# Loading ScalarE's function tables ahead of a step's waits instead of behind them

## The reference

```
x = x + tanh(g_xattn[0]) * L0_xattn(layernorm(x), ctx)   # top-32-of-77 cross attention, 4 heads; FiLM; a state-space
                                                         # convolution over 512 positions; a GELU network; layer norms
x = x + tanh(g_ffn[0])   * L0_ffn(layernorm(x))          # two butterfly networks with a GELU between them
x = x + tanh(g_xattn[1]) * L1_xattn(layernorm(x), ctx)   # softmax attention, 16 heads of 8
x = x + tanh(g_ffn[1])   * L1_ffn(layernorm(x))          # 8 experts, best 2 of them, silu(u) * v
return x
```

## Time and profile before

| | |
|---|---|
| median of 3 runs | 367.29 us (366.8 to 367.44) |
| span of the profiled execution, first to last instruction | 365.1 us |
| mean granted TensorE clock in it | 0.911 of full speed |
| busy: PE, DVE, ACT, POOL | 298.4, 262.1, 209.0, 138.0 us |
| table loads on ACT | 28, together 35.9 us |

### The profile page before, as it was taken

How to read it: one execution, slowest core, us unless ns; L and a number is a source line. 1 busy time by engine, 2 the same in 40 slices (tenths; PEclk the granted TensorE clock), 3 DMA queues, 4 the chain that set the end, 5 groups by cost and what they waited for, 6 DMA issues and landing times.

```text
span 365.1 us, 5331 instructions
## 1 busy us (share of the span) xinstructions
PE 298.4 (82%) x1518; PEld 149.1 (41%) x1518; DVE 262.1 (72%) x1201; ACT 209.0 (57%) x430; POOL 138.0 (38%) x212
## 2 busy tenths in 40 slices
PE   1652100779997899999789999989999999899995
PEld 0320000639654357544544542544432444532541
DVE  3998599999799999679998882586413458801762
ACT  3799851062225465597535486544786945575560
POOL 0398998488874935443165007140000000000000
PEclk9995555658969999999999999999999999999998
DMA  7960000000000000000000000000000000000001
GB/s 246 415 238 0 1 1 0 4 1 2 0 1 1 3 0 2 2 0 1 0 2 1 1 0 2 0 2 1 0 2 0 0 3 29 0 2 3 29 19 39
DMA packets 2912, 9.56 MB, mean 26 GB/s; under 512 B 579, under 2 KB 580, under 8 KB 2628
## 3 DMA queue, kind: packets, MB, share of 16 engines
q1 hardware_dynamic: 2884, 9.23, 6.7%
HBM read 8.18 MB, written 1.05 MB: 25 GB/s over the span
## 4 chain that ended last, share of the span: by engine, by line
PE 57%; DVE 28%; POOL 6%; ACT 5%; issue 2%; DMA 1%; POOLq 0%; DVEq 0%; ACTq 0%
PE bank L461 56%; DVE R L1128 8%; DVE V L1119 5%; DVE arena L1034 4%; DVE MT L1034 3%; ACT arena L781 2%; POOL MT L1399 2%; POOL AO L1399 1%; DVE KT L1353 1%; POOL arena L1399 1%; ACT RS L781 1%; ACT L778 1%; DVE arena L1042 1%; DVE XG L1042 1%; DMA pack_kgen<-in_kgen 1%
## 5 line engine op out<-in xcount | busy, mean ns | idle before, releaser
L781 ACT ACTIVATE arena<-bank 128x512 f32<-128x512 f32 (+3 forms) x75 | 38.4, 572 | 22.3 <-PE bank L461 13.4
L778 ACT ACT_TABLE_LOAD x28 | 35.9, 1283 | 25.0 <-PE bank L461 14.0
L1128 DVE MATCH_REPLACE8 R<-V,R 128x77 f32<-128x77 f32 x192 | 40.5, 221 | 0.0
L461 PE MATMUL bank<-LO,pack_first 128*128 128x512 f32 x48 | 28.1, 677 | 15.0 <-ACT LO L781 15.0
L1456 POOL TENSOR_SCALAR sel<-R 128x308 f32<-128x308 f32 x16 | 17.7, 1107 | 37.8 <-DVE R L1128 33.1
L1119 DVE MAX8 V<-R 128x8 f32<-128x77 f32 x192 | 31.2, 223 | 0.0
L1092 DVE TENSOR_REDUCE pack_bfly<-bank 128x4 f32<-128x308 f32 x64 | 26.0, 468 | 7.2 <-PE bank L461 7.1
L461 PE MATMUL bank<-M,XN 128*128 128x308 f32 x32 | 12.8, 485 | 21.1 <-DVE XN L1034 19.8
L461 PE MATMUL bank<-arena,pack_dft 128*128 128x256 f32 (+1 forms) x96 | 29.2, 454 | 0.1
L781 ACT ACTIVATE E<-bank,negm 128x77 f32<-128x77 f32 x64 | 15.4, 326 | 15.9 <-DVE negm L1038 15.9
L781 ACT ACTIVATE LO<-bank 128x512 f32<-128x512 f32 x20 | 12.0, 600 | 21.6 <-PE bank L461 21.6
(11 more groups left out here) (208 smaller groups left out, 714.0 us busy)
## 6 DMA issues: line engine op xcount, KB each, us to landing
pack_bfly<-in_bfly SPq DMA_DIRECT2D x1, 2420.0 KB, 10.3
pack_dft<-in_dft SPq DMA_DIRECT2D x1, 1536.0 KB, 13.8
X<-in_x SPq DMA_DIRECT2D x4, 256.0 KB, 12.4
out_x<-X SPq DMA_DIRECT2D x4, 256.0 KB, 2.0
pack_ffn<-in_ffn SPq DMA_DIRECT2D x1, 512.0 KB, 14.3
pack_first<-in_first SPq DMA_DIRECT2D x1, 474.0 KB, 5.0
pack_moe<-in_moe SPq DMA_DIRECT2D x1, 452.0 KB, 15.7
pack_att<-in_att SPq DMA_DIRECT2D x1, 413.0 KB, 15.2
```

The lines of the kernel that those rows point to most:

```text
L461: return nc.tensor.matmul(out, lhsT, rhs, start=start, stop=stop, **kw)
L778: nc.scalar.add_instruction(mybir.InstLoadActFuncSet(name=nc.get_next_instruction_name(), act_func_set_id=need, ins=[], outs=[]))
L781: return nc.scalar.activation(out, in_, func, **kw)
L1128: nc.vector.match_replace(R8[:, g % 2, r % 2, h, :], V8[:, g % 2, h, r, :], src, NEG)\
```

## The change

Each step of ScalarE gets, before its waits are emitted, the table of its first function that needs one. `leads` names that function for the steps that have one; the part of `a` that loads a table becomes a function `have`, which is called at the head of each step and still from `a`. `s_cols` (Tanh), `s_kgen0` (Exp) and `units1` (Silu) are not found in `leads`, so a load that they need stays where it was.

```diff
             table = [None]
 
-            def a(out, in_, func, **kw):
+            leads = {"var": ACT.Ln, "score": ACT.Exp, "keyA": ACT.Exp, "normA": ACT.Ln, "top2": ACT.Exp,
+                     "ffn_up": ACT.Gelu, "fold_up": ACT.Gelu, "units0": ACT.Silu, "s_trig": ACT.Tanh,
+                     "s_qsin": ACT.Sin, "s_psin": ACT.Sin, "s_qexp": ACT.Exp, "s_pexp": ACT.Exp}
+
+            def have(func):
+
                 need = table_of.get(func, table[0])
                 if need != table[0]:
                     nc.scalar.add_instruction(mybir.InstLoadActFuncSet(
                         name=nc.get_next_instruction_name(), act_func_set_id=need, ins=[], outs=[]))
                     table[0] = need
+
+            def a(out, in_, func, **kw):
+                have(func)
                 return nc.scalar.activation(out, in_, func, **kw)
...
                 tile = int(step[-1]) if step[-1].isdigit() else 0
                 g = NT * b + tile
+                have(leads.get(step if step in leads else step.rstrip("012345")))
                 if step == "center2":
```

## The result

The changed kernel takes 364.2 us (median of 14 runs, 363.48 to 367.79), the kernel before in the same sitting 367.12 us (14 runs, 366.66 to 369.76). The ratio, which goes by all runs and not by the two medians, is 0.9939, with a 95% interval of 0.9912 to 0.9965: 2.2 us faster, give or take 1.0. The medians lie 2.9 us apart, because eight runs of the changed kernel took 363.5 to 364.3 us and six took 366.1 to 367.8, while 13 of the 14 of the kernel before took 366.7 to 367.7. Forecast were 1.11 us and 366.2 us, with a range of 364.8 to 367.4. The direction was right and the size too small. The profiled execution spans 361.7 us, 3.4 us less than that of before.

The account below looks back on a forecast made before the run. PE was taken to bound the kernel, busy 82% of the span, with few table loads on the last chain. Gains of 1.00 and 0.11 us made 1.11 us: 367.29 to 366.2 us, range 364.8 to 367.4.

Parts of the forecast that it names:

- Site 1: Load at 313.42, keyA0 of batch 2: hidden in ACT's 2.04 us wait, PE's expand of batch 1 gains 1.00 us.
- Site 2: Load at 141.51, score2 of batch 2: PE's idft wins 0.43 us but then waits for DVE; nothing (bounds 0 and 0.43).
- Site 3: Tail, top2 and units0 of batch 3: both loads moved, PE's transposes of the gates 0.11 us earlier (bounds 0 and 0.11).
- The other loads: The other 12 loads: nothing, those after 189 lying under a PE without a gap; uncovered, each at most 1.28 us.
- Rival 1: Last four PE passes: three or four run at full clock, 1.2 to 1.6 us more gain, 364.6 to 365.0 us; 12%.
- Rival 2: Between 316 and 348: a DVE or ACT run not hanging on PE covers the gain, 366.8 to 367.3 us; 17%.
- Rival 3: Tail passes from 352.30 on: clock falls earlier, 0.42 us per pass, up to 4.2 us, 370.4 us, slower; 8%.
- Rival 5: Table switches on ACT: each holds ACT longer than its record, hidden in idle time before; 366.8 us; 3%.

Follow-up runs that it names:

- keyA alone: Changed kernel with only the keyA entry left in `leads`, so two loads move, those at 269 and 313; 365.01 us, ratio 0.9932 to the kernel before.
- the tail alone: Changed kernel with only top2 and units0 loading ahead of their waits (five loads); 366.9 us, ratio 0.9988 to the kernel before.
- small fill: One matmul of 512 columns, read by nobody, added in PE's last pause: on the kernel before 366.16 us, on the changed kernel 363.72 us.
- a load too many: Changed kernel with one extra load of an unused table ahead of the load of keyA0 of batch 2; 365.46 us, ratio 0.9953 to the kernel before.
- four entries of thirteen: Changed kernel with only keyA, ffn_up, top2 and units0 loading ahead of their waits; 363.70 us, ratio 0.9926 to the kernel before.
- ffn_up alone: Changed kernel with only ffn_up loading ahead of its waits (four loads); 366.44 us, ratio 0.9974 to the kernel before.
- everything but keyA: Changed kernel with the loads of keyA back behind their waits; 366.5 us, ratio 0.9995 to the kernel before.
- units1: Changed kernel with units1 (Silu) added to `leads`, moving the load at 287 too; 364.15 us, ratio 0.9945 to the kernel before.

## Why the prediction was right in direction and short in size

*Site 1, the term that carried the forecast.* The mechanism was right in each part: the load right behind the copy, 0.75 us of idle time left, expand 1.01 us earlier for 1.00. The term was mis-sized behind it. I had let the score passes of scoreA3 "follow PE at 1.00 us earlier". But they wait for exponentials two to four as well, and those came the full 1.28 us earlier; in the trace of before they, and not PE's pace, had released the later passes: the third matmul of scoreA3 and the pass at 316.84 start right after the fourth exponential, whose bank that matmul takes, ends at 316.77 (314.71 and 2.06 us). So PE won 0.22 us more there (316.84 to 315.12 is 1.72, 0.22 over the 1.50 at expand), and the site is worth 1.22 us. keyA alone repeats it: 1.00 us at expand, 1.21 us behind it. I had worked out the release of the first bank and taken it for all four.

*Site 2.* Right. PE wins its 0.43 us, and DVE's run takes them back, in the timeline of PE and then of DVE after:

```profile
142.40 1.02 PE L461 MATMUL bank<-LO,pack_first 128*128 128x512 f32 x2
143.26 3.62 PE L461 MATMUL bank<-pack_dft,arena 128*128 128x256 f32 x16
...
147.98 1.13 PE L461 MATMUL bank<-X,pack_first 128*128 128x512 f32 x2 [0.21 <-DVE X L1051]
149.31 1.13 PE L461 MATMUL bank<-XG,pack_first 128*128 128x512 f32 x2
```

```profile
148.56 0.69 DVE L1043 TENSOR_TENSOR XG<-XG,XN 128x512 f32<-128x512 f32 x1
```

idft starts 0.66 us earlier (143.92 to 143.26), of which 0.22 are the scatter that was there before. The step at 149.31 is 0.22 us earlier, as DVE's product at 148.56 is the earlier trace rows, and a new wait of 0.21 us for DVE stands at 147.98.

*Site 3.* Right: 0.11 us, and 0.12 with the tail alone.

*The other loads.* Here a step failed: "nothing" for the load at 209.71, because PE is busy 47.40 of 47.40 us around it and each shape keeps its own spacing. It hid 0.3 us. Matmuls on few rows run beside each other in these traces (four passes of 12 rows with 0.38 us each take 0.56 us together), so records of two shapes overlap and cover a wait of one of them. Here the wait was that of the fourth matmul of 32 rows for its bank, and it was passed on: at 213.97 three passes of 12 rows, then one of 32 rows at 214.01 with 0.59 us, and the fourth of 12 rows only at 214.44. There was no gap in the busy time, and the four passes took 0.85 us from start to end; with the loads of ffn_up moved they take 0.56 (213.95).

*Rivals.* Rival 1 came true in the profiled execution, on top of the forecast. Its price was right (1.2 to 1.6 us said, 1.52 measured), and by the rows its chance of 12% was low. The fact to hold against "the fall may move with PE's own work" stood in the trace: it came within 0.3 us of the step's start, and the forecast moved that start by over 1 us. Rival 2 did not happen: DVE idles 0.54 us at 315.32 for 0.52 worked out. ACT idles the same 1.36 us at 316.81 as before, where I had 0.36 us left: I had moved PE earlier and left ACT's own exponentials where they were, though they moved by more than PE did. Rival 3 did not happen in the changed kernel's profile, but the profile of the changed kernel with the small fill has it, a stretch at a clock of 0.50 from 350.5 to 353.8 (stretch, length, PE busy, clock, DMA share, GB/s, PE alone):

```profile
350.50:353.80 3.30, 3.30 (x5) 0.50 0.00 0
...
359.70:361.60 1.90, 1.90 (x5) 1.00 0.00 0
```

So it was a case with weight. Rival 5 is out by the run with a load too many.

*The sum.* The parts that the runs bear out are 1.22 at site 1, 0.3 at 214 us and 0.11 in the tail, 1.6 us, against 1.11 forecast. The runs measured 2.2 us (1.3 to 3.2). The rest of the best estimate is the last step's clock, in some share of the executions, and scatter. That the clock has a part in it is likely: the larger group of the changed kernel's runs lies 3 us below that of the kernel before, which is near 1.6 and 1.5 us together, and the other group overlaps it and brings the 3 us down to 2.2. But the runs carry no record of the last step, so how often it counts stays open. That the result by the ratio falls inside the range is no merit of the sum: the range went so far down for rival 1.

## What to carry to other kernels

A function-table load behind a wait costs its 1.28 us only where another engine stands behind the work that follows it: of 28 loads one site gave nearly all, and four entries of thirteen gave as much as all. When one release moves, work out every release behind it: four exponentials freed four banks, and PE gained 0.22 us more behind the later ones than behind the first. Where PE's matmuls on few rows run beside each other, "busy without a gap" does not exclude a wait: measure a step from its first start to its last end and compare it with its sisters.

## What was not expected of the hardware

The granted clock falls in the last step in one set of kernels and not in another. In the profiles with site 1 as before and no fill it falls in four of four (the kernel before, the tail alone, ffn_up alone, everything but keyA: 3.48, 2.77, 3.25 and 3.28 us for the four passes). With site 1 moved and no fill it stays up in six of six (1.95 to 1.96 us). The pause ahead of the step is 0.94 us in the rows of both sets, so the pause alone does not decide, though filling it did keep the clock up on the kernel before. What differs is site 1 itself and with it the moment at which the step comes. Counted from the start of the trace the moment does not sort the ten: units1 begins the step at 359.72 and keeps the clock, between the tail alone (359.20) and everything but keyA (360.58), which lose it. Counted from the last rise of the clock ahead of the tail it does: the step begins 248.2, 248.7 and 248.9 us after the rise where the clock falls and 247.1 to 247.5 us where it stays, and in the two traces with one more stretch at 0.50, 238.4 us against 237.1. The rise is read from a stretch across it, in the trace of before at 109.58, where the microsecond from 109 to 110 has a mean of 0.71:

```profile
109.00:110.00 1.00, 1.00 (x3) 0.71 0.00 0
```

Which of the two decides, site 1 or the moment, was not told apart, and the cause stays open. A pause is not needed either: in the changed kernel with the small fill the clock falls at 350.4, ahead of the fill, with PE busy throughout (the rows under rival 3).

Executions also differ in where the clock falls early on. Stretches (stretch, length, PE busy, clock, DMA share, GB/s, PE alone) of the kernel before, then of the one with units1, then of the kernel before with the small fill, all of them ahead of any edit that bears on PE:

```profile
102.80:109.50 6.70, 6.70 (x11) 0.50 0.00 1
119.20:122.60 3.40, 2.39 (x9) 1.00 0.01 2
```

```profile
119.20:122.60 3.40, 3.21 (x6) 0.50 0.00 0
```

```profile
72.00:88.00 16.00, 13.39 (x105) 0.50 0.01 2
102.80:109.50 6.70, 6.70 (x28) 1.00 0.00 1
116.00:122.60 6.60, 5.20 (x9) 0.50 0.01 2
```

Executions of the changed kernel lie between 363.5 and 367.8 us, a wider spread than the change is worth. That such stretches make it is likely, from rows like these: the traces of two executions of 366.6 us, that with units1 and that with the small fill, have a stretch at 0.50 that the trace of the 363.5 us execution has not. It is not shown, since few executions have a trace. It is why a difference between two traces has to be read step by step, from the nearest common point on.
